# The last layer's projection as seven products of halves instead of eight blocks

## What is computed

```python
xr = jnp.einsum('nd,rdf->rnf', x, W)      # x: elu of the layer before; 3 relations, 768 x 768 each
qi, kj = xr[etype, dst] @ q, xr[etype, src] @ k
alpha = leaky_relu(qi + kj, 0.2)
e = exp(alpha - segment_max(alpha, dst)[dst])
a = e / (segment_sum(e, dst)[dst] + EPS)
out = segment_sum(a * xr[etype, src], dst) + b
```

## Time and profile before

| | us |
|---|---|
| median of 3 runs (1998.45 to 2000.24) | 1998.51 |
| the profiled execution | 2000.49 |
| its span in the profile | 1998.7 |
| PE busy / DVE busy / ACT busy, of the span | 1842.2 / 1489.9 / 716.3 |
| projection phase of the last layer, from the first load's issue to the last store's landing | 1386.26 to 1640.46 |
| attention phase, the rest | 1640.46 to 1998.7 |

### The profile page before, as it was taken

One profiled execution on the slowest core, in us unless ns is written; L12 is line 12 of the kernel. 1 busy time (PEld: TensorE's weight loads), 2 busy tenths in 40 slices (PEclk: granted clock), 3 DMA queues, 4 the chain that ended last, 5 costly groups with the idle time before them and its releaser, 6 DMA issues. The chain is left out here.

```text
span 1998.7 us, 22525 instructions
## 1 busy us (share of the span) xinstructions
PE 1842.2 (92%) x7830; PEld 1275.1 (64%) x7831; DVE 1489.9 (75%) x2741; ACT 716.3 (36%) x1202; POOL 19.7 (1%) x38
## 2 busy tenths in 40 slices
PE   5789978679999899999699999998999979999997
PEld 3445544379944455555499999997655545555554
DVE  7869867789766663999699999995146027988996
ACT  5758965444213321111243434342311111322331
POOL 0000001010000000000000000000000000000000
PEclk9889999889999899999899999998999999999999
DMA  6200039652062316453322212112165437677764
GB/s 163 78 5 26 30 116 314 203 174 58 21 184 90 126 72 226 141 206 115 101 66 74 81 59 83 59 56 80 64 200 190 179 113 242 212 254 248 249 217 164
DMA packets 148943, 266.70 MB, mean 133 GB/s; under 512 B 11647, under 2 KB 118006, under 8 KB 145498
## 3 DMA queue, kind: packets, MB, share of 16 engines
q1 hardware_dynamic: 109002, 201.40, 30.6%
q10 hardware_dynamic: 36560, 49.66, 7.3%
q0 software_dynamic: 3264, 14.16, 2.5%
HBM read 209.46 MB, written 55.71 MB: 133 GB/s over the span
## 5 line engine op out<-in xcount | busy, mean ns | idle before, releaser
L1095 PE MATMUL ps<-work 128*128 128x193 f32 (+1 forms) x3200 | 531.0, 330 | 32.8 <-DVE work L1845 32.8
L1095 PEld LDWEIGHTS ps<-work 128*128 128x128 f32 x3200 | 530.4, 191 | 33.9 <-issue 33.9
L1045 PE MATMUL ps<-work 128*128 128x384 f32 (+2 forms) x1440 | 473.7, 490 | 5.7 <-ACT work L1303 2.6
L1045 PEld LDWEIGHTS ps<-work 128*128 128x128 f32 x1440 | 273.6, 191 | 197.1 <-issue 17.0
L1118 PE MATMUL ps<-work 128*128 128x384 f32 (+1 forms) x1050 | 341.2, 488 | 10.3 <-DVE work L1951 10.3
L1464 ACT ACTIVATE work<-work,s 128x1280 f32<-128x1280 f32 x160 | 218.0, 1363 | 293.4 <-DVE work L1839 293.3
L1118 PEld LDWEIGHTS ps<-work 128*128 128x128 f32 x1050 | 200.0, 191 | 151.5 <-issue 12.4
L1839 DVE SCALAR_TENSOR_TENSOR work<-work,sd 128x1280 f32<-128x1280 f32 x160 | 247.7, 1549 | 38.6 <-PE ps L1095 25.7
L1845 DVE SCALAR_TENSOR_TENSOR work<-work,counts 128x1280 f32<-128x1280 f32 x160 | 237.8, 1486 | 2.7 <-ACT work L1464 2.6
L1611 DVE TENSOR_SCALAR work<-work,winoff 125x480 bf16<-125x480 f16 x480 | 158.0, 401 | 0.1
L866 PE MATMUL ps<-work 125*128 125x480 bf16 x480 | 116.4, 393 | 33.3 <-ACT work L1208 16.2
(11 more groups left out here) (220 smaller groups left out, 1539.6 us busy)
## 6 DMA issues: line engine op xcount, KB each, us to landing
work<-hs_d SPq DMA_DIRECT2D x75, 960.0 KB, 5.3
work<-pqrow_d SPq DMA_DIRECT2D x18, 1280.0 KB, 6.4
work<-nomask_d SPq DMA_DIRECT2D x70, 320.0 KB, 3.3
nomask_d<-work SPq DMA_DIRECT2D x40, 320.0 KB, 6.8
hx_d<-work ACTq DMA_DIRECT2D x60, 192.0 KB, 1.9
work<-hx_d SPq DMA_DIRECT2D x120, 96.0 KB, 1.9
hs_d<-counts ACTq DMA_DIRECT2D x45, 192.0 KB, 2.0
feat<-srow_d SPq DMA_DIRECT2D x3, 2560.0 KB, 12.5
```

The lines of the kernel that those rows point to most:

```text
L1045: last = mm(bank(n % 4 if i else n % 2, cols), xT[:, j, t * P:(t + 1) * P], wv[:, j, :], start=(j == 0), stop=(j == DT - 1))
L1095: last = mm(sums_at(c, t, u), xe[i % RING][:, t * P:(t + 1) * P], hx[:, i % RING, 0:1 + c.width], start=(r == 0 and k == 0 and t % TB == 0 ...
```

## The change

The projection, too, is made with seven products of halves. For relation r and column half h (six *units*, `UNITS`) and pair p of row tiles (five), a *round* q = 5u + p takes the 256 rows of tiles p and p + 5, the 768 features as two halves of 384, and 192 columns of W's left half with 192 of its right half. Each of the seven products is three float32 products of 128 x 128 by 128 x 192 (198 for four of them in the first unit). There are 30 rounds.

- **x's sums** (`x_sums`): four DVE operations of 384 columns for each pair of tiles, once. **W's sums** (`w_sum`): four DVE operations of 576 columns for each unit.
- **Sums in the banks.** A round has three banks, X, Y and Z, two sets of them in turn. X takes P1; ACT copies it out (`keep_a`); P6 is added in the same bank; ACT copies it (`keep_b`); P7 is added; ACT copies it (`keep_c`); P4 is added, which makes C21 (`fetch_c21`). Y takes P2 and gives C11 = Y + P1. Z takes P5 and gives C22, then P3 is added, and gives C12. DVE makes C11, C22, C12 and two differences (`c11`, `c22`, `c12`).
- **The order on PE** interleaves two rounds: P1(q), P7(q-1), P2(q), P4(q-1), P5(q), P3(q-1), P6(q).
- **The stores**: the five blocks of a round (`blocks`, two buffers) go out as one DMA of 480 KB in 640 pieces of 768 bytes. W comes in four DMAs a unit, in pieces of 768 bytes.
- The elu, turning and copying of x's tiles are spread over the first four rounds, in the order 0, 5, 1, 6, 2 and so on. The searches begin at round 8, two a round, and the masks have two buffers. The `pq_all` loads of relations 1 and 2 are issued in the attention phase, behind the second and the fifth `hs_d` load.

```diff
@@ -121,6 +121,17 @@
 PRODUCTS = "P1 P2 P6 P7 P5 P3 P4".split()
 A_SLOTS, H_SLOTS, H_PITCH = 4, 4, 386
 SPARE = 3
+
+
+QH, QE = FH // 2, FH // 2 + 6
+UNITS = [(r, h) for r in range(RELS) for h in range(2)]
+ROUNDS = len(UNITS) * TH
+TILES_D = [t + half * TH for t in range(TH) for half in range(2)]
+ORDER_D = [(q + late, name) for q in range(ROUNDS + 1)
+           for late, name in ((0, "P1"), (-1, "P7"), (0, "P2"), (-1, "P4"), (0, "P5"), (-1, "P3"), (0, "P6"))
+           if 0 <= q + late < ROUNDS]
+DONE_D = {key: i + 1 for i, key in enumerate(ORDER_D)}
+S_ROUND, MAX_ROUND, PQ_ROUND = 6, 8, 25
...
+            def pq_rows_d(ci, s, r):
+                for q in range(2):
+                    row = 24 * ci + 2 * r + q
+                    sp.dma_start(pq_all[r][q], pqrow_d[row:row + 1, :].rearrange("h n -> (h n)").partition_broadcast(P)) \
+                        .then_inc(s.pq_in[r % 2].sem, 16)
...
+                for n in range(2):
+                    mask_load(n)
+                sp.wait_ge(srow_out, 16 * ci)
+                s_load(0)
...
@@ -669,6 +735,8 @@
                     for g in range(TH):
                         for m in range(STEPS_D):
                             h_load(g * STEPS_D + m)
+                            if g == 0 and m in (1, H_SLOTS):
+                                pq_rows_d(ci, s, 1 if m == 1 else 2)
                             if m == OUT_AT:
                                 if g:
...
+                    u, p = q // TH, q % TH
+                    low, high = slice(p * P, (p + 1) * P), slice((p + TH) * P, (p + TH + 1) * P)
+                    b11, t1, b21, b22 = (raw[u % 2][:, k, c, :, :] for k in range(2) for c in range(2))
+                    t2, t3, t4 = wsum
+                    x_bank, y_bank, z_bank = (3 * (q % 2) + i for i in range(3))
+                    ext = u == 0 and name in ("P1", "P2", "P5", "P4")
+                    if name == "P1":
+                        at, left, right, start = x_bank, xT[:, 0:3, low], b11, True
+                        if p == 0:
+                            pe.wait_ge(*s.w_in[u % 2].at(64 * (u // 2 + 1)))
...
+                            pe.wait_ge(d_c21, q - 1)
+                            pe.wait_ge(d_c12, q - 1)
+                    elif name == "P2":
+                        at, left, right, start = y_bank, xT[:, 3:6, low], b21, True
+                        if q >= 2:
+                            pe.wait_ge(d_c11, q - 1)
+                    elif name == "P5":
+                        at, left, right, start = z_bank, xs[0][:, :, low], t1, True
...
+                    elif name == "P4":
+                        at, left, right, start = x_bank, xT[:, 3:6, high], t4, False
+                        pe.wait_ge(d_c, q + 1)
+                        if p == 0:
+                            pe.wait_ge(d_w, 4 * u + 4)
+                    else:
+                        at, left, right, start = z_bank, xs[2][:, :, low], b22, False
+                        pe.wait_ge(d_c22, q + 1)
...
+                    for j in range(3):
+                        last = mm(bank(at, n_), left[:, j, :], right[:, j, 0:n_], start=(start and j == 0), stop=(j == 2),
+                                  skip_group_check=True)
+                    last.then_inc(d_prod, 1)
...
+                for q, name in ORDER_D:
+                    product(q, name)
+                    for part, after in enumerate(("P1", "P4")):
+                        round_ = q + part
+                        if name == after and round_ < TH - 1 and (part == 0 or round_):
+                            turn(2 * round_ + 2 + part)
+                        if name == after and round_ == S_ROUND:
...
+                def w_load(u):
+                    r, h = UNITS[u]
+                    for k in range(2):
+                        for c in range(2):
+                            cc = c * FH + h * QH
+                            act.dma_start(raw[u % 2][:, k, c, :, 0:QH],
+                                          t_in["w_d"][r * D + k * FH:r * D + (k + 1) * FH, cc:cc + QH].rearrange("(j p) c -> p j c", p=P)) \
+                                .then_inc(s.w_in[u % 2].sem, 16)
+
...
+                def fetch_c21(q):
+                    act.wait_ge(d_prod, DONE_D[q, "P4"])
+                    if q >= 2:
+                        act.wait_ge(d_blk_out[q % 2], 16 * (q // 2))
+                    nc.scalar.activation(blocks[q % 2][:, 1, :], bank(3 * (q % 2), QH), ACT.Copy).then_inc(d_c21, 1)
+
+                def store(q):
+                    (r, h), p = UNITS[q // TH], q % TH
+                    m = r * TH + p
+                    act.wait_ge(d_blk, q + 1)
+                    act.wait_ge(d_c21, q + 1)
+                    act.dma_start(hs_d[m * P:(m + 1) * P, :].rearrange("p (b h c) -> p b h c", b=5, h=2)[:, :, h, :],
+                                  blocks[q % 2]).then_inc(d_blk_out[q % 2], 16)
...
+
+                w_load(0)
+                for e in range(3):
+                    elu_exp(e)
+                fetch_turned(0)
+                elu_exp(3)
+                fetch_turned(1)
+                for q in range(ROUNDS + 1):
+                    if q < ROUNDS:
+                        keep_a(q)
+                    if q < TH - 1:
+                        fetch_turned(2 * q + 2)
+                    if q == S_ROUND:
+                        copy_rows(srow_t, ci, RELS, srow_c, 0)
+                    if q == PQ_ROUND:
+                        copy_rows(pq_t, ci + 1, 2 * RELS, pq_c, 0)
+                    if q:
+                        keep_c(q - 1)
+                        fetch_c21(q - 1)
+                    if q < TH - 1:
+                        fetch_turned(2 * q + 3)
+                    for e in range(2 * q + 4, min(2 * q + 6, T)):
+                        elu_exp(e)
+                    if q == S_ROUND:
+                        copy_rows(srow_t, ci, RELS, srow_c, 1)
+                        nc.scalar.activation(s02[:, :, 0:RELS], sd[:, :, 0:RELS], ACT.Copy, scale=0.2)
+                    if q == PQ_ROUND:
+                        copy_rows(pq_t, ci + 1, 2 * RELS, pq_c, 1)
+                    if q >= 2:
+                        store(q - 2)
+                    if q < ROUNDS:
+                        keep_b(q)
+                    if q == TH - 2:
+                        w_load(1)
+                    if q >= TH and q % TH == 0 and q // TH + 1 < len(UNITS):
+                        act.wait_ge(d_prod, DONE_D[q - 1, "P3"])
+                        w_load(q // TH + 1)
+                store(ROUNDS - 1)
+                for i in range(2):
+                    act.wait_ge(d_blk_out[i], 16 * (ROUNDS // 2))
...
-                def store_sums(n):
-
-                    r, t = n // (2 * T), n % T
-                    act.wait_ge(d_turned, r * T + t + 1)
-                    q, p = t // TH, t % TH
-                    act.dma_start(block_d(r, p, 2 + 2 * q), keep[q][p]).then_inc(keep_out[q][p], 16)
-
...
+                def c11(q):
+                    y_bank = 3 * (q % 2) + 1
+                    dve.wait_ge(d_prod, DONE_D[q, "P2"])
+                    dve.wait_ge(d_a, q + 1)
+                    if q >= 2:
+                        dve.wait_ge(d_blk_out[q % 2], 16 * (q // 2))
+                    if q < TH:
+                        v.tensor_tensor(sd[:, q, 0:6], bank(y_bank, 6, QH), part_a[q % 2][:, QH:QE], ALU.add)
+                    v.tensor_tensor(blocks[q % 2][:, 0, :], bank(y_bank, QH), part_a[q % 2][:, 0:QH], ALU.add).then_inc(d_c11, 1)
+
...
+                def c12(q, made):
+                    x_bank, z_bank = 3 * (q % 2), 3 * (q % 2) + 2
+                    if q < TH:
+                        dve.wait_ge(d_c21, q + 1)
+                        dve.wait_ge(s_dve, made)
+                        ins = v.tensor_tensor(sd[:, q + TH, 0:6], bank(x_bank, 6, QH), ext_sb, ALU.add)
+                        if q == TH - 1:
+                            ins.then_inc(sd_done, 1)
+                    dve.wait_ge(d_prod, DONE_D[q, "P3"])
+                    dve.wait_ge(d_b, q + 1)
+                    v.tensor_tensor(c12_sb, bank(z_bank, QH), part_b[q % 2][:, 0:QH], ALU.add).then_inc(d_c12, 1)
+                    dve.wait_ge(d_c12, q + 1)
+                    v.tensor_tensor(blocks[q % 2][:, 2, :], c12_sb, blocks[q % 2][:, 0, :], ALU.subtract)
+                    v.tensor_tensor(blocks[q % 2][:, 4, :], blocks[q % 2][:, 3, :], c12_sb, ALU.subtract).then_inc(d_blk, 1)
...
+                for q in range(ROUNDS + 1):
+                    u, p = q // TH, q % TH
+                    new_unit = q < ROUNDS and u and p == 0
+                    for e in range(2 * q + 2, min(2 * q + 4, T)):
+                        up(e)
+                        if e + 2 < T:
+                            low(e + 2)
+                    if new_unit:
+                        w_sum(u, 1)
+                    if q:
+                        next_made = c22(q - 1)
+                    if new_unit:
```

(62 more changed lines are left out.)

348 lines of the change are left out of this document (234 added, 114 removed).

## The result

The changed kernel takes 2054.22 us (median of 4 runs, 2048.03 to 2056.07), the kernel before 1998.48 us (4 runs, 1997.89 to 2000.24). The ratio is 1.0272, with a 95% interval from 1.0248 to 1.0296: 55 us slower. The profiled execution took 2052.43 us with a span of 2050.6; before, it was 2000.49 us.

What follows compares the result with a forecast made beforehand. The prediction took a ring through the store's landing to bound the projection. Its terms, 8.1 + 12.3 + 10.0 + 29.2 + 10.4 + 201.6 + 14.7, gave 286.3 us, 32 more than before: 2030 us, range 1999 to 2062.

Steps and rivals of the forecast that it cites:

- The ring: Projection rounds: four products, C21's copy, store landing, `c11`, `c12`, next P1; 5.05 us plus the landing, against 6.83 of PE work.
- W and the ramp: Start of the projection: W's first load 8.1 us, then rounds 0 to 4 at 12.3, 10.0, 14.6, 14.6 and 10.4.
- Rounds 5 to 28: 24 rounds of 8.15 us, plus 3.8 for sums of W and 2.2 for rows of scores: 201.6 us.
- The period: Time from one round's P1 to the next: 5.05 us plus the store's landing, 8.15 us.
- L: Landing time of a round's 480 KB store in 640 pieces, priced from trace rows at 3.1 us.
- rival 3: Landing is longer, 4.3 us, by mask and weight loads sharing the engines: 34 us more, 2064; chance 0.14.
- The end: From P1(29) to the last landing: 6.83 + 3.0 + 0.7 + 1.0 + 3.1 = 14.7 us.
- Rival 2: Landing as short as the old stores', 2.0 us: 31 us less, 2000, no change; chance 0.06.
- the fitted rule: Skill's 2.0 us + bytes / 436 GB/s, for another issuing path: 3.1 us for this store, 2.6 with its offset taken off.
- Rival 1: PE sets the projection's pace, the store late or its landing hidden: phase 239 us, 15 less, 1983; chance 0.10.
- Rival 4: PE's clock falls to 0.50 at each round's pause: up to 3.9 us more, 27 times, up to 2135; chance 0.05.
- What was costed at nothing: Searches run in DVE during PE's products; `pq_all` loads moved into the attention are covered by the ring of four slots.

Runs made afterwards that it cites:

- e4: The changed kernel with masks from the third on and W from the third unit on loaded with 16 columns a row only: 2034.54 us.
- e10: Changed kernel, store issued behind P1's copy, P1 freed of `c12` past the score columns, W's loads one a round, DVE's order in rounds 0 to 3 changed: 1984.06 us.
- e3: The changed kernel with each round's store going out as 128 pieces of 3840 bytes: 2040.73 us, ratio 1.0220 to before.
- e7: The changed kernel with the store issued behind P1's copy and W's four loads of a unit issued one a round: 1994.46 us, ratio 1.0001 to before.

## Why the prediction was right or wrong, point by point

**The mechanism: right.** The ring by P4, C21's copy, the store, the landing, `c11` and `c12` sets the pace; two cuts of it at two places bring 44 and 40 us. PE's waits, DVE's waits and their releasers are those named. Not all its signs came as stated: P1 was to wait 1 to 1.5 us, and did so in nine of the 25 rounds from the fifth on; in fifteen it waited 1.6 to 4.7.

**The size: 24 us too small** (2030 for 2054.2; the phase 286.3 for 309.8). The prediction's last step adds 32.3 where its sum gives 286.3 - 254.2 = 32.1, which changes nothing. Term by term:

- *W and the ramp* up to P1(5), forecast 8.1 + 12.3 + 10.0 + 29.2 + 10.4 = 70.0; measured 1446.67 - 1381.33 = 65.3. W was there at 1387.65 when DVE began its first sum, 6.3 us after the first issue and not 8.1; round 2 took 12.4 and not 14.6; round 3 took 14.6 and round 4 10.2, as forecast. The granted clock was 0.80 up to there.
- *Rounds 5 to 28*, forecast 201.6; measured 1675.23 - 1446.67 = 228.6. This is the term that failed, 27 us in three pieces:
  - The period: 8.31 for 8.15, 3.9 us over 24 rounds. By the round shown above: from P1's start to the copy 4.18 (forecast 3.9), from there to the issue 0.06, since the issue doesn't wait for the copy to end (0.3), L 3.18 (3.1), from the landing to the next P1 0.88 (0.7 and the hand-overs, 0.15).
  - Long landings: the 24 stores on the chain took 91.1 us, 14.8 more than 24 of 3.18. Eleven took 3.17 to 3.20, thirteen 3.5 to 6.7. The prediction named this in one sentence ("mask loads and weight loads can lengthen it"), gave it to rival 3, and put zero into the sum, though it counted two mask loads a round in rounds 8 to 22, 15 of these 24. e4 shows the cause for most of it: with small loads 10.0 of the 14.8 us went, and the four long landings that stayed are beside the first two masks, which e4 leaves whole, and beside broadcasts.
  - The low clock behind the four longest: 8.2 us (below).
- *The end*: 15.9 for 14.7. In all -4.7 + 27.0 + 1.2 = 23.5.

**A price from undisturbed rows** was thus used for a transfer that is disturbed in over half of its rounds. The longest landing in rounds 5 to 28, 6.67 us, began at 1535.02; the timeline shows what was issued in front of it:

```profile
1532.73 0.32 SPq L582 DMA_DIRECT2D feat<-nomask_d  x1
1534.38 0.32 SPq L582 DMA_DIRECT2D counts<-nomask_d  x1
1534.74 0.43 SPq L585 DMA_DIRECT2D feat<-srow_d  x1
1535.02 0.52 ACTq L1491 DMA_DIRECT2D hs_d<-counts  x1
```

1.3 MB in three loads on SP's queue, and the store on ACT's among them. With both masks cut to 16 columns (e4) the landing here still took 6.05.

**The landing, L = 3.1: right** at 3.2, and so was its working: 37 ns a packet for 39, 0.52 us for the issue, and with 128 pieces 2.5 us. Rival 2 (2.0) falls. So does the smaller L of 2.6 that would have followed from the fitted rule with its offset taken off. The rule itself, which knows bytes alone, gives 3.1 for both layouts; the runs have 3.2 with 640 pieces and 2.5 with 128, so its 3.1 is near by chance.

**Rival 1 (PE sets the pace): false** for this kernel, and its 239 us for the phase are near the 241.7 that e10 reaches. e10 gets there with the store off C21's back, P1 free of `c12`, the loads of W spread and the ramp reordered. That the two numbers lie so near is in part luck: the rival had 12 us for the waits and the clock of a ramp that e10 doesn't have, and e10 has a landing of 10.8 us that the rival doesn't.

**Rival 3 (L = 4.3 on average)** was right in kind. The average landing in rounds 5 to 28 is 91.1 / 24 = 3.8, halfway between the forecast's and the rival's; the clock does the rest.

**Rival 4 (low clock in every round): false, but not idle.** Between 1650.28 and 1675.23 PE pauses for 1.3 us every 8.3 and is granted all of the clock; behind a long pause it is not:

```profile
1650.28:1675.23 24.95, 21.20 (x126) 20.40 (x127) 4.81 (x16) 3.97 (x12) 0.00 (x0) 1.00 0.29 97
1602.00:1606.00 4.00, 3.65 (x11) 3.68 (x12) 3.74 (x7) 0.33 (x1) 0.00 (x0) 0.50 0.68 199
```

The first six instructions of P1 tell the clock: 1.21 us at full clock. From P1(5) to P1(29) there are 25 pauses; the 21 of up to 2.53 us leave it at 1.21 or 1.22, the four of 2.71, 3.31, 3.46 and 4.73 don't:

```profile
1466.43 1.21 PE L1113 MATMUL ps<-feat,work 128*128 128x192 f32 x6 [2.53 <-DVE counts L1991]
...
1502.90 2.26 PE L1113 MATMUL ps<-work 128*128 128x192 f32 x6 [3.31 <-DVE counts L1991]
...
1542.58 2.26 PE L1113 MATMUL ps<-feat,work 128*128 128x192 f32 x6 [4.73 <-DVE counts L1991]
...
1563.43 1.76 PE L1113 MATMUL ps<-feat,work 128*128 128x192 f32 x6 [2.71 <-DVE counts L1991]
```

Their pieces of 24 instructions took 5.64, 6.27, 5.83 and 7.09 us in place of 4.15, 8.2 us in all. So these late landings were paid twice: once as a pause, and again in the clock behind it.

In this one trace it looks as if the size of the pause decided. The others don't bear that out. These two rows are from e3:

```profile
1594.50 1.21 PE L1113 MATMUL ps<-work 128*128 128x192 f32 x6 [2.71 <-DVE counts L1991]
...
1613.01 1.95 PE L1113 MATMUL ps<-work 128*128 128x192 f32 x6 [1.93 <-DVE counts L1991]
```

The pause of 2.71 us leaves the clock at its upper level, the one of 1.93 doesn't. Over the ten traces of the new kernels, all 14 pauses of 3.3 us or more between P1(5) and the end of the phase have the low clock behind them; of those between 1.9 and 2.8 us ten have it and 29 don't. What decides between them stays open. The Trainium skill, "TensorE: Matmul & The Clock Gate", section "HAM oscillation — how this bites in real kernels", has PE go cold in each wait for a DMA, in a kernel whose waits are of some 3 to 5 us. The traces agree for waits of that size; in the changed kernel, most of whose waits are shorter, it happened in four of 25.

**What was costed at nothing** stayed near nothing: with the moved `pq_all` loads PE's pause at the start of the attention is 11.2 us, where it was 10.3, and the attention lasts 358.1 to 359.5 us in the ten traces of the new kernels, where it lasted 358.2. The searches run in DVE's idle time.

**What stays open:** of the 27 us, the 14.8 and 8.2 are read from the chain of one execution. e4 took masks and weights away together, and not the broadcasts, so the share of masks alone and of weights alone wasn't tried apart in the changed kernel; nor was the clock without the pauses.

## What to carry to other kernels

When a change puts a store's landing on a ring (a buffer is written again only after the store out of it has landed, and what waits for it feeds the matmuls), count the ring's period before the engines' work, and price the landing in the traffic it will meet, not from rows in which it is alone. Issue the store as soon as its data exist, not behind the copy of a later round, but look at what it then stands behind in its own queue. A pause of PE of 3.3 us or more was paid twice in every trace here, for itself and for the clock after it; one of 1.9 to 2.8 us only sometimes.

## What the runs showed of the hardware

- A store of 480 KB landed in 3.2 us in 640 pieces of 768 bytes and in 2.5 us in 128 pieces of 3840; its issue took 521 ns and 326 to 345 ns (medians).
- The same store took 8.6 us right behind 1.18 MB of loads in its own queue, with mask loads on the other, and 9.6 to 10.8 us issued within 3.4 us behind 2.4 MB on the other queue (two broadcasts of 640 KB, two masks, a load of biases), with or without a load of W: three times the undisturbed landing. I had counted on 4.3 (rival 3) and on under 5 (e7).
- Behind each of 14 pauses of 3.3 us or more the clock was granted at 0.50. Behind shorter ones it was so sometimes: after one of 1.93 us (e3), and not after one of 2.71 in the same trace.
- The part of the program ahead of the phase, with the same code, ended anywhere within 10.5 us in the profiled executions. Phases are therefore compared by their length, not by where they end.
